# A three-stage kernel (RWKV projections, experts, output) as three programs, and as one with early starts of the next stage

## The reference, cut to what matters

```python
# attention branch (RWKV)
prev = shift(xn); xx = prev - xn
r, k, v = (xn + xx*tm_r) @ Wr.T, (xn + xx*tm_k) @ Wk.T, (xn + xx*tm_v) @ Wv.T
g = sigmoid((xn + xx*tm_g) @ Wg.T)
# scan over time: a, b <- w*a + exp(k)*v, w*b + exp(k)
wkv = (a + exp(u)*exp(k)*v) / (b + exp(u)*exp(k))
attn_out = layernorm((sigmoid(r) * wkv * g) @ Wo.T) * ln_g + ln_b
# mixture-of-experts branch
z = w_norm * rmsnorm(xn)                 # 4096 tokens
w, sel = top_k(softmax(z @ w_router), 4) # 32 experts, at most 256 tokens each
y[e] = (silu(z[e] @ w_gate[e]) * (z[e] @ w_up[e])) @ w_down[e]
out  = sum over the 4 of w * y + sigmoid(z @ w_shared_gate) * shared_mlp(z)  # hidden size 1408
result = x + attn_out + xn + out
```

## Time and profile before

| | us |
|---|---|
| three runs | 1799.75, 1800.13, 1804.7 (median 1800.13) |
| the profiled execution | 1803.59 |
| its span, first to last instruction | 1801.8 |
| TensorE busy | 1687.4 (94%) |
| VectorE busy | 1247.5 (69%) |
| GpSimd busy | 874.2 (49%) |
| ScalarE busy | 661.2 (37%) |

### The profile page before, as it was taken

The page is one execution under the profiler, slowest core; times in us unless marked ns, Lnnn a source line. Parts: engine busy times, 40 slices in busy tenths (PEclk is TensorE's granted clock), DMA queues, the critical chain, the costliest instruction groups (busy, mean ns, idle before and its releaser), DMA issues. The chain is left out here.

```text
span 1801.8 us, 26943 instructions
## 1 busy us (share of the span) xinstructions
PE 1687.4 (94%) x8752; PEld 1445.2 (80%) x8752; DVE 1247.5 (69%) x1798; ACT 661.2 (37%) x1083; POOL 874.2 (49%) x727
## 2 busy tenths in 40 slices
PE   4899999999599999999986889999999999999998
PEld 4687887778489999999974778888788888888887
DVE  4888787888255555555545868778686868777776
ACT  3444445444256656656642322112121211212121
POOL 2678777777634444454423524344252524334251
PEclk9999999999889999999998999999999999999999
DMA  6233334333366676676637655455454443343431
GB/s 222 94 137 129 133 140 160 120 117 117 120 249 217 242 249 221 234 251 228 228 110 263 211 203 170 156 187 172 165 165 140 151 147 106 113 163 117 141 107 51
DMA packets 130475, 299.43 MB, mean 166 GB/s; under 512 B 23692, under 2 KB 35212, under 8 KB 129872
## 3 DMA queue, kind: packets, MB, share of 16 engines
q1 hardware_dynamic: 110928, 264.64, 41.5%
q0 software_dynamic: 19456, 33.67, 6.6%
HBM read 233.64 MB, written 81.36 MB: 175 GB/s over the span
## 5 line engine op out<-in xcount | busy, mean ns | idle before, releaser
L738 PE MATMUL pj<-mix,w 128*128 128x512 f32 x1536 | 368.4, 397 | 18.6 <-POOL mix L311 18.4
L738 PEld LDWEIGHTS pj<-mix,w 128*128 128x128 f32 x1536 | 287.6, 190 | 85.2 <-POOL mix L311 14.6
L1616 PE MATMUL s_gp<-s_zT,s_wg 128*128 128x512 f32 x1056 | 263.7, 400 | 37.6 <-DVE s_wg L1524 21.9
L1616 PEld LDWEIGHTS s_gp<-s_zT,s_wg 128*128 128x128 f32 x1056 | 203.9, 194 | 84.4 <-DVE s_wg L1524 24.8
L1630 PE MATMUL s_yp<-s_wd,s_h 128*128 128x512 f32 x1056 | 255.2, 391 | 2.9 <-DVE s_h L1433 2.9
L1616 PE MATMUL s_up<-s_zT,s_wu 128*128 128x512 f32 x1056 | 253.7, 389 | 0.0
L1630 PEld LDWEIGHTS s_yp<-s_wd,s_h 128*128 128x128 f32 x1056 | 199.2, 189 | 44.7 <-issue 3.3
L1616 PEld LDWEIGHTS s_up<-s_zT,s_wu 128*128 128x128 f32 x1056 | 198.2, 188 | 41.4
L876 POOL TENSOR_TENSOR e_wg<-e_g_in,e_wg 128x1408 fp32r<-128x1408 f32 x32 | 103.4, 3233 | 214.6 <-ACT e_wg L896 214.6
L311 POOL TENSOR_TENSOR mix<-mixf,mix 128x512 fp32r<-128x512 f32 x128 | 175.8, 1403 | 61.1 <-ACT mix L385 60.9
L1275 POOL DMA_INDIRECT s_picked<-y_rows,s_slot x128 | 143.4, 1121 | 85.0 <-DVE s_total L1483 47.4
(11 more groups left out here) (148 smaller groups left out, 2377.5 us busy)
## 6 DMA issues: line engine op xcount, KB each, us to landing
s_wu<-wu_split SPq DMA_DIRECT2D x77, 512.0 KB, 3.5
e_g_in<-in_w_gate SPq DMA_DIRECT2D x32, 704.0 KB, 4.5
e_u_in<-in_w_up SPq DMA_DIRECT2D x32, 704.0 KB, 5.9
zT_tiles<-zT SPq DMA_DIRECT2D x32, 512.0 KB, 2.6
e_d_in<-in_w_down SPq DMA_DIRECT2D x32, 512.0 KB, 6.8
y_rows<-e_y SPq DMA_DIRECT2D x32, 512.0 KB, 2.9
s_zT<-zT_tiles SPq DMA_DIRECT2D x32, 512.0 KB, 5.6
x_in<-in_x SPq DMA_DIRECT2D x32, 256.0 KB, 4.1
```

The lines of the kernel that those rows point to most:

```text
L738: last = pe.matmul(pj[m][:], w[i][:, w_part, k, m * P:(m + 1) * P], mix[:, i % 2, k, x_part, :], start=(k == 0 and q == 0), stop=(k == KC ...
L1616: last = pe.matmul(bank[:], parts[w_part][:, k, :], zT[:, :, x_part, k, :], start=(q == 0 and k == 0), stop=(q == 2 and k == KC - 1))
```

## The change

One block holds all three stages. Every SBUF tensor is placed at an address by hand, the eight PSUM banks are shared, and each stage hands functions to the one before it, which calls them in its last rounds:

- last projection round: SyncE loads expert 0's weights; ScalarE and VectorE split them (GpSimd the gate's low part); all 16 scatters follow V's low parts on GpSimd, and VectorE makes the low parts of R and G; TensorE turns expert 0's rows ahead of the last k of project G.
- expert 30 and 31: SyncE loads pieces 0, zT, the norm vectors, then the first wkv data and pieces 1; pieces 0 are split during expert 31.
- output stage, first round: pieces come two ahead, GpSimd makes the low parts of U as well as of down, Wo comes in four tensors instead of one staged in `total`.
- in every projection round: `choose(b + 1)` moves from after V's mixes of round b + 1 to ahead of the gates 0 and 1 of round b; `assign` moves to directly behind V's mixes; `count` to between the halves of K; the scatters are spread as 3, 2, 4, 2, 5, all ahead of K's low parts.

```diff
@@ project_stage, SyncE @@
             if before:
                 store_gate(b - 1)
+            if not more:
+                first_weights()
@@ project_stage, GpSimd @@
                 for k in range(KC):
                     mix_lo(b, V_, k)
-                for k in range(KC):
-                    mix_lo(b, R_, k)
-                scatter(b, 0, 4)
-                for k in range(KC):
-                    mix_lo(b, G_, k)
-                scatter(b, 4, 12)
-                if more:
-                    for k in range(KC):
-                        mix_lo(b + 1, K_, k)
-                scatter(b, 12, 16)
+            if not more:
+                scatter(b, 0, NT * TOPK)
+                return
+            scatter(b, 0, 3)
+            mix_lo(b, R_, 0)
+            mix_lo(b, R_, 1)
+            scatter(b, 3, 5)
+            mix_lo(b, R_, 2)
+            mix_lo(b, R_, 3)
+            scatter(b, 5, 9)
+            mix_lo(b, G_, 0)
+            mix_lo(b, G_, 1)
+            scatter(b, 9, 11)
+            mix_lo(b, G_, 2)
+            mix_lo(b, G_, 3)
+            scatter(b, 11, 16)
+            for k in range(KC):
+                mix_lo(b + 1, K_, k)
@@ project_stage, VectorE @@
                 for k in range(KC):
                     make_mix(b, half, V_, k)
-                choose(b)
-                if not before:
+            if before:
+                assign(b)
+            else:
                     weight_lo(R_)
...
+            if not more:
+                for k in range(KC):
+                    mix_lo(b, R_, k)
                 make_ekv(b, 0)
                 make_ekv(b, 1)
...
+            if not more:
+                for k in range(KC):
+                    mix_lo(b, G_, k)
+                first_weights()
...
                     make_mix(b + 1, 1 - half, K_, 0)
                     make_mix(b + 1, 1 - half, K_, 1)
+                choose(b + 1)
                 make_gate(b, 0)
                 make_gate(b, 1)
@@ project_stage, TensorE @@
                 project(b, K_, 0)
+            if before:
+                count(b)
                 project(b, K_, 1)
...
-                project(b, G_, 1)
+            project(b, G_, 1, None if more else first_turn)
@@ expert_stage, SyncE @@
+        def first_weights():
+            sp.wait_ge(shared["scores_made"], B * NT)
+            for i in range(2):
+                sp.wait_ge(shared["z_stored"][i], 16 * B * NT // 2)
+                sp.wait_ge(shared["zT_stored"][i], 16 * B * NT // 2)
             load(0, 0)
+
+        def read_table():
+            sp.wait_ge(shared["scattered"], 16 * B * NT * TOPK)
+            sp.dma_start(table[:], d["table"]).then_inc(table_loaded, 16)
+
+        def main(*early):
+            output_early.extend(early)
             sp.wait_ge(gathered[0], 32)
+            sp.wait_ge(shared["g_done"], B * KC)
             load(1, 1)
             experts(sp, one_expert)
@@ expert_stage, GpSimd @@
+        def main(early):
+            output_early.append(early)
+            gate_lo(0, 0)
+            gather(0, 0)
+            gather(1, 1)
             experts(pool, one_expert)
@@ output_stage, SyncE @@
+        def during_last():
+            sp.wait_ge(shared["e_y_done"], (E - 1) * NCT)
+            load_wkv(0, 0)
             load_x(0, 0)
+            for which in (G, U, D):
+                load_piece(which, 1)
+            store_wu(0)
+            load_gate(0, 0)
             load_wkv(0, 1)
...
+                    if f + 2 < NFS:
                             for which in (G, U, D):
-                                load_piece(which, f + 1)
+                            load_piece(which, f + 2)
+                    if f + 1 < NFS:
+                        store_wu(f + 1)
@@ output_stage, GpSimd @@
                     if 1 <= f <= 6:
                         gather(b, f + 1)
+                if zero(b) and f + 2 < NFS:
+                    weight_lo(U, f + 2)
+                    weight_lo(D, f + 2)
@@ output_stage, ScalarE @@
                     elif more:
                         silu(b + 1, 1 - half, 0)
+                if zero(b) and f + 2 < NFS:
+                    for which in (G, U, D):
+                        weight_hi(which, f + 2)
+                if zero(b) and f == 1:
+                    act.wait_ge(wo_loaded, 64)
+                    for m in range(KC):
+                        act.activation(wo[m][:, 0, :], wo_in[m][:], ACT.Copy).then_inc(wo_hi, 1)
@@ output_stage, VectorE @@
                     hidden_lo(b, half, f)
                     fill(f)
+                if zero(b) and f + 2 < NFS:
+                    gate_lo(f + 2)
+                if zero(b) and f in (2, 3):
+                    out_lo(2 * f - 4)
+                    out_lo(2 * f - 3)
```

## The result

| | us | ratio to before, 95% interval |
|---|---|---|
| kernel before, median of 4 runs beside it | 1801.03 | |
| changed kernel, median of 4 runs (1772.45 to 1773.06) | 1772.74 | 0.984 (0.9823 to 0.9857) |
| its profiled span | 1770.9 | |
| forecast | 1738.5, range 1716 to 1757 | |

The change makes the kernel 28 us faster; 62 were forecast. TensorE is busy 1690.1 us (1687.4 before): what changed is where it stands still. The traces differ by 30.9 us and the medians by 28.3, because the profiled execution of the kernel before took 1803.59 us.

The account below looks back on a forecast made before the run. TensorE's own work plus holes at two seams, the first output round and steady projection rounds bound the kernel; 27 (seam 1) + 38.5 (seam 2, first output round) - 3.8 (projection) = 61.7 us, from 1800.13 to 1738.5, range 1716 to 1757.

Parts of the forecast that it names:

- seam 1: Between projection and experts: first expert product at about E + 2, 27 us gained in sum, bounds 22 and 30.
- the second seam and the first output round: From last expert matmul to first output projection: 97 us after the change, gain 38.5 us, bounds 20 and 46.
- E: End of the last projection matmul, 473.94 us in the kernel before; steps of seam 1 are counted from it.
- Round 0 gets choose earlier, in front of V: 1 us: First projection round: the choice of experts ahead of V was to cost 1 us, within 3.8 us net lost.
- sixteen scatters at the spacing of the train take 20.5, so they end near E - 12: Last projection round, GpSimd: scatters spaced 1.28 us (0.97 and 0.30 idle) take 20.5 us and end near E - 12.
- E': In the changed kernel, where the projection's products would end undisturbed, 483.7 us; the counterpart of E.
- Hidden; without that cover up to 2 us: Seam 1: expert 1's weights, loaded after E in 9.7 us and wanted 13.6 us after the first product, cost nothing.
- the 97 us of the first output round: Output projection starts 97 us after 937.3, the last expert matmul's end: VectorE's 94.8 plus 2 for waits that do not mesh.
- 80.0 + 7.1: First output round, VectorE busy: 80.0 us left without U's 11 low parts, plus 7.1 from GpSimd operations added.
- 7.7 + 2: First output round, VectorE idle: 7.7 us for 11 turns through ScalarE, 2 us for waits that do not mesh.
- The contention term: First output round: 11 added GpSimd operations of 1.29 us, one half of their time put on VectorE, 7.1 us.
- The rival of full exclusion: First output round: VectorE and GpSimd exclude each other entirely, 14.2 us on VectorE, 7 more, 1745.5 us; chance 0.2.

Follow-up runs that it names:

- the old order: Changed kernel with choose, count, assign, routing exponentials and scatters of the projection stage back where they stood before the change: 1773.21 us, ratio 0.9836.
- one experiment: Changed kernel with VectorE's eight low parts for R and G in the last projection round cut to 16 of 512 columns: 1772.77 us, ratio 0.9845.
- the experiment with small parts: Changed kernel with GpSimd's up and down low parts of tiles 2 to 10, first output round, cut to 16 of 512 columns: 1758.0 us, ratio 0.9767.
- the one where the pause moved: Changed kernel with two more GpSimd scatters in round 0, into a table that nobody reads: 1773.44 us, ratio 0.9836.

## Why the prediction was wrong, step by step

Of the 30.8 us that are missing between the forecast (61.7) and the traces (30.9), 16.5 are missing at seam 1, 11.6 at the second seam and the first output round, and 5.9 in the projection stage; 3.5 that were not forecast come back in the later rounds.

**Right.**
- Seam 2: the gate product follows the last down product directly; 15.4 us gone.
- Steady rounds: no hole ahead of V, one of 0.73 us at K released by VectorE's gate and GpSimd's low part (1 to 2 forecast), one of 0.72 at z, a round of 54.1 us (54 forecast). The sizes were smaller than mine, both of them: the two holes cost 1.45 us a round where I had 2.9, and the gain, those 1.45 and the 0.45 by which a round got shorter, was 1.9 where I had 3.2. That the round came out right is in part luck.
- Transposes, rows and copies behind the last scatter: 13.3 us to the first expert product; my steps from E - 12 to E + 2 make 14. The table took 2.8 us, not 4.7, and the rows 2.5 from issue, not 5.7; the transposes to the product took 4.3 at a granted clock of 0.72, not 3. So the near agreement of the sum is in part luck too: steps that were too long and too short cancel.
- The direction, and that VectorE would release what is late in the first output round.

**Wrong: "Round 0 gets choose earlier, in front of V: 1 us".** By the first transposes of round 1 it was 11.8. (The rest of the stage, 2.8 lost in my sum, gained 2.1, which by luck hides part of this.) I worked out one steady round and applied it to the first, where the change leaves other steps in their old places. Two edits meet there. The choice (5.3 us of VectorE) came ahead of V's mixes with nothing to hide it, and V started 5.3 us later. And GpSimd's scatters came ahead of R's low parts while the assignment that they wait for stayed behind two splits of weights: a wait of 12.85 us. The experiments give 6.9 of the time back by undoing both. Of what remains, K's hole in round 1 is the choice of round 1 in front of the gates (seen in the trace, not tried alone), and the 2.8 us that the old order has in the one program stay open.

**Wrong: "sixteen scatters at the spacing of the train take 20.5, so they end near E - 12".** They began where I said (452.22, E' - 31.5) and ended at E' - 3.7: 27.8 us. 5.0 are a pause between the first two; one experiment shows it to be none of the doing of VectorE's low parts, another that it goes with the count of scatters; 2.7 are scatters that took 1.2 to 2.0 us in place of 0.97. The trace of before held the pause, at the same scatter:

```profile
457.59 1.26 POOL L319 DMA_INDIRECT slot_tokens<-token,slot  x1 [2.94 <-issue]
```

I took the spacing from two neighbours of the train and not its whole length.

**Wrong: "Hidden; without that cover up to 2 us".** Expert 1's weights cost 6.5 us by the time, 8.5 in the traces. I let their load start at E; it started at E' + 11.7, because on SyncE it stands behind the wait for expert 0's gather and behind the last gate store. I had noted that the SiLU of expert 0 queues behind the split of these weights and took the cover as given. With the load early expert 0 took 13.6 us, the figure of the prediction. Expert 0 took 8.5 us more than forecast, and its first product came 7.6 us later behind the projection than forecast (E' + 9.6, not E + 2): together 16.1 of the 16.5 us that seam 1 fell short (27 - 10.5).

**Wrong by size: the 97 us of the first output round.** It took 108.7. VectorE was to be busy 80.0 + 7.1 and idle 7.7 + 2; it was busy 91.98 and idle 16.7. The contention term was built on one half of each GpSimd operation; the experiment with small parts shows that VectorE's own work is at most 72.8 us, so contention was at least 19.2, more than the 14.9 us by which GpSimd's busy time fell; why more is not shown. My 80.0, taken from before, already held some 7 us of it, as its trace shows for the hidden low parts alone (VectorE, 952.7 to 1072.8; with GpSimd's subtractions gone eleven of them take 7.6 us):

```profile
L1433 DVE TENSOR_TENSOR s_h<-s_act_g,s_h 128x512 fp32r<-128x512 f32 x11 | 14.6, 1331 | 3.1 <-ACT s_h L1359 3.1
```

The idle time had two waits I had left out, 5.2 us for the clearing of the picked rows and 3.3 for the gate weights' copies. The rival of full exclusion named the right mechanism; by size it too fell short (104 against 108.7). That moving U to GpSimd would be no relief, as that rival had it, is what the run with U back on VectorE shows: 7 us better. The rule of the Trainium skill cited there ("SBUF — State Buffer", section Who interferes with whom) names an exclusive lock, and the traces agree with it in direction: a hidden low part takes 1502 ns beside GpSimd's subtractions and 692 ns without them.

**Not forecast.** From the first output projection to the last the changed kernel needs 706.1 us, the kernel before 709.7. All but 0.6 us of this is one round, 105.2 us before and 102.3 after; why it got shorter was not tried.

## What to carry to other kernels

A reordering worked out on a steady round must be worked out again on the first and the last, where its neighbours stand elsewhere; all that was lost in the projection stage was lost in rounds 0 and 1. An instruction moved on a queue should be followed to the wait in front of it and to everyone behind it: scatters in front of low parts, a load behind a wait and a store, a choice in front of a gate cost 2.7, 6.5 and 10.7 us. And where VectorE is the limit, subtractions of two SBUF operands moved to GpSimd were no relief here but a loss; try such a move both ways.

## What the runs showed of the hardware

- GpSimd pauses at its 114th scatter: 2.94 us where the DMA queues were empty when the scatter before it moved (in the kernel before, in the one with the old inner order, and in the one where the pause moved), 5.26 us where expert 0's weights and a store of ek of 1 MB filled them. The DMA queues of the changed kernel (packets, MB, share of the engines), from 450 to 455 and from 455 to 456 us:

```profile
q1 hardware_dynamic: 859, 2.01, 102.3%
...
q0 software_dynamic: 29, 0.00, 2.0%
```

  The packets of the first scatter, issued at 452.22, move from 455 us on, when the others begin to thin out (78.5% in that microsecond), and the second scatter is issued some 2 us behind them. That the pause is a wait for earlier transfers to land is read from this and not tried. In the changed kernel the gathers of picked rows pause by 2.21 us at their 114th and by 1.09 at their 50th.
- In the first output round 14.9 us less of GpSimd's busy time took 19.2 us off VectorE's, and a subtraction that takes 0.69 us with GpSimd's subtractions gone took 1.5 on the mean beside them.
- Beside VectorE's splits of expert 0's weights a scatter took 2.02 us in place of 0.97 (seen in the traces with those splits, not tried by leaving them out).
- A wait of TensorE at a seam costs twice: the down product of expert 0 took 7.20 us behind a wait of 5.13 (granted clock 0.56 from 508.0 to 515.4 us), and 4.38 without one.
